# Two expert groups on one core: who loads group 1's gate and up weights, and when

## The chip, the cores and the metric

One core of one Trainium2 chip runs the whole program. The metric is the device time of one execution in microseconds, and the median of the runs counts. Lower is better.

## The reference

The program is a model of two layers on x of 2 x 2048 tokens by 256 channels, all in float32. The change lies in the first layer's feed-forward part, a mixture of experts in two groups of 32 experts each. Cut to what matters:

```python
def _moe_group(x2, router_w, wg, wu, wd, top_k):       # x2: 4096 x 256, top_k = 2
    scores = softmax(x2 @ router_w)                    # 32 experts
    expert_weights, expert_indices = lax.top_k(scores, top_k)
    order = argsort(flat_e); xs = x2[tok]              # 8192 rows sorted by expert
    gate = lax.ragged_dot(xs, wg, group_sizes)         # wg, wu: 32 x 256 x 128
    up = lax.ragged_dot(xs, wu, group_sizes)
    ys = lax.ragged_dot(silu(gate) * up, wd, group_sizes)   # wd: 32 x 128 x 256
    return zeros.at[tok].add(ys * flat_w[order])

out0 = _moe_group(x2, router_w0, wg0, wu0, wd0, 2)
out1 = _moe_group(x2, router_w1, wg1, wu1, wd1, 2)
out = (out0 * 2 + out1 * 2) / 4
```

Before it stand a layer norm and an attention, behind it the second layer: a gated delta attention with an MLP, and a soft mixture of experts.

## The kernel before

The kernel is written in phases. Each phase is a block in which every engine has its own program; the next phase begins when all five engines have come to the end of it. Engines talk through semaphores that count upwards.

Each group of experts is one phase, `phase_experts` with g = 0 and g = 1. The tokens of a group lie in DRAM in `slots_x`, sorted by expert and padded so that a tile of 128 rows belongs to one expert. There are always N = 96 tiles: 8192 / 128 = 64, and one more for each of the 32 experts. `tile_expert` holds the expert of each tile, which is known only at run time. Every expert has at least one tile, so tile t belongs to an expert not above t; and expert e can still own tile 64 + e but no later one.

A tile passes through the engines as follows (line numbers are the profile's). SyncE loads x for four tiles at once, 512 KB, into `xs`, which has room for eight (L1447). TensorE transposes a tile (L1514), ScalarE copies it from PSUM (L1547), TensorE multiplies by the expert's gate and up weights in `w_gu` (L1523), ScalarE applies silu (L1551), VectorE multiplies by up (L1570), TensorE transposes again (L1530), VectorE copies (L1574), TensorE multiplies by the down weights (L1536), ScalarE copies to `y` (L1560), and SyncE stores four tiles at once (L1456).

`staged` skews the steps of a tile over successive rounds: in round r TensorE does the first step of tile r, the second of tile r − 1, and so on. Some rounds at the start and the end are written out one by one, with constants as tile numbers; those between run in a hardware loop whose body holds `unroll` rounds, 8 on TensorE. How many rounds stand written out at the start is normally the number of stages less one, 3 on TensorE; the argument `alone` sets another number, and in group 1 TensorE has `alone=E + 1`, 33.

There is one buffer `w_gu` (8 MB over all partitions) for both groups. Group 0's content is loaded long before, in `phase_route` (L1378). Group 1's content is loaded in group 1's own phase by SyncE: `load_chunk` (L1439) loads four experts with 4 DMAs of 256 KB; there are 8 chunks. `load` issues chunk 0 behind the x load of tiles 0 to 3, and chunks 1 to 7 behind the x load of tiles 4 to 7, so that SyncE's program order is: x load, 4 weight DMAs, x load, 28 weight DMAs, x load, and so on. TensorE waits for chunk t / 4 ahead of the gate-up of tiles 0, 4, 8 to 28, which it can do because these rounds are written out.

The down weights have a buffer each. Group 1's go into `z_sb`, in one DMA of 4 MB that GpSimd issues in group 0's phase (L1472), after it has scattered group 1's tokens to `slots_x` with 64 indirect DMAs (L1352), which begin when tile 20 of group 0 has passed. Behind that DMA GpSimd's program for group 0 ends. In group 1's phase GpSimd gathers group 0's results, 64 indirect DMAs with a multiplication and an addition each (L1479, L1486, L1491).

Of the kernel before, what the change touches and what calls it, by code (L numbers as in the profile page):

```python
# [989 lines left out]
def phase_route(nc, sems, x, o_sb, out_w, out_b, routers, x1_sb, xn_sb, lg_sb, top_val, top_idx, ident,  # L990
# [3 lines left out]
    with Phase(nc, "route", sems) as ph:  # L994
# [42 lines left out]
        @block.sync  # L1037
        def _(sp):
            x_landed.prime(sp)
            sp.dma_start(w_in[:, :, :], out_w.rearrange("(c p) d -> p c d", p=P)).then_inc(consts_in, 16)  # L1040
            sp.dma_start(bias[:, 0, :], row_broadcast(out_b)).then_inc(consts_in, 16)
            for g, r in enumerate(routers):
                sp.dma_start(r_w[:, :, g * E:(g + 1) * E], r.rearrange("(k p) e -> p k e", p=P)).then_inc(consts_in, 16)

            def load(t, p):
                sp.wait_ge(x1_ready.sem, x1_ready.before(t))
                hold(sp, gate)
                sp.dma_start(x_in[:, p, :, :], x[bass.ds(t * GP, GP), :].rearrange("(n q) c -> q n c", q=P)).then_inc(x_landed.sems[p], 32)
            staged(sp, N, load)
            load_gate_up(sp, w_gu, *first_experts[:2], w_landed)  # L1050

        @block.gpsimd
        def _(pool):
# [325 lines left out]


CHUNK = 4
BACKS = 6
LOOPS_RUNNING = 20


def phase_experts(nc, sems, g, w_gu, w_d, next_w_d, weights, next_down, w_landed, down_landed, xn_sb, pos, scattered,
                  slots_x, slots_y, tile_expert, x1_sb, weight, ident):


# [5 lines left out]
    with Phase(nc, f"experts{g}", sems) as ph:  # L1395
# [12 lines left out]
        if g:  # L1408
# [1 line left out]
            back_landed = [ph.sem(f"back_landed{i}", soft=True) for i in range(BACKS)]  # L1410
            back_scaled = ph.sem("back_scaled")
            back_added = ph.sem("back_added")
        chunk_landed = [ph.sem(f"chunk_landed{c}") for c in range(E // CHUNK if g else 0)]
        x_landed = ph.transfers("x_landed")
        turned = ph.steps("turned", ahead=2 * GT)
        x_ready = ph.steps("x_ready")
# [11 lines left out]
        def _(sp):  # L1428
# [3 lines left out]
            if not g:  # L1432
                sp.dma_start(w_d[:, :, :], wd.rearrange("e h d -> h e d")).then_inc(down_landed[g], 16)

            def load_chunk(c):
                own = slice(c * CHUNK, (c + 1) * CHUNK)
                for k in range(KD):
                    for i, w in enumerate((wg, wu)):
                        sp.dma_start(w_gu[:, k, own, i, :],  # L1439
                                     w[own, k * P:(k + 1) * P, :].rearrange("e p h -> p e h")).then_inc(chunk_landed[c], 16)  # L1440

            sp.wait_ge(scattered[g], 16 * SCATTERS)

            def load(t, p):
                sp.wait_ge(turned.sem, turned.at(t * GT - GT - 1))
                hold(sp, gate)
                sp.dma_start(xs[:, p * GT:(p + 1) * GT, :],  # L1447
                             slots_x[bass.ds(t * GP + base, GP), :].rearrange("(n q) c -> q n c", q=P)).then_inc(x_landed.sems[p], 32)
                if g and isinstance(t, int) and t < 2:
                    for c in range(1) if t == 0 else range(1, E // CHUNK):  # L1450
                        load_chunk(c)

            def store(t, p):
                sp.wait_ge(y_ready.sem, y_ready.at(t * GT + GT - 1))
# [10 lines left out]
        def _(pool):  # L1465
            if g == 0:
                scatter_tokens(pool, 0, SCATTERS_EARLY, SCATTERS, xn_sb, pos, slots_x, scattered[0])

                pool.wait_ge(h_t_ready.sem, h_t_ready.at(LOOPS_RUNNING))
                scatter_tokens(pool, 1, 0, SCATTERS, xn_sb, pos, slots_x, scattered[1])  # L1470
                pool.wait_ge(scattered[1], 16 * SCATTERS)
                pool.dma_start(next_w_d[:, :, :], next_down.rearrange("e h d -> h e d")).then_inc(down_landed[1], 16)  # L1472
                return

            def fetch(i):
# [25 lines left out]
        def _(pe):  # L1501
            for s in (turned, gated, h_turned, down):
                s.prime(pe)
            if not g:
                pe.wait_ge(w_landed, 16 * 2 * KD)
            pe.wait_ge(down_landed[g], 16)

            def expert(t):
# [7 lines left out]

            def gate_up(t, p):
                e = expert(t)
                if g and isinstance(t, int) and t < E and t % CHUNK == 0:
                    pe.wait_ge(chunk_landed[t // CHUNK], 16 * 2 * KD)  # L1520
                pe.wait_ge(x_ready.sem, x_ready.at(t))
                for k in range(KD):
                    mm = pe.matmul(ps_g[p % 2][:, 0:2 * HID], x_t[:, p % 2, k, :],  # L1523
                                   w_gu[:, k, bass.ds(e, 1), :, :].rearrange("q a i h -> q (a i h)"),
                                   start=(k == 0), stop=(k == KD - 1))
                mm.then_inc(gated.sem, 1)
# [5 lines left out]
            def go_down(t, p):  # L1532
# [2 lines left out]
                pe.wait_ge(y_ready.sem, y_ready.before(t, 2))  # L1535
                pe.matmul(ps_y[p % 2][:, 0:D], h_t[:, p % 2, :], w_d[:, bass.ds(e, 1), :].rearrange("q a c -> q (a c)"),  # L1536
                          start=True, stop=True).then_inc(down.sem, 1)
            staged(pe, N, turn_x, gate_up, turn_h, go_down, unroll=2 * GT, alone=E + 1 if g else None)

        @block.scalar  # L1540
        def _(act):
# [1860 lines left out]
def two_layers(nc, t, out):  # L3402
# [13 lines left out]
    with ExitStack() as sems, ExitStack() as whole:  # L3416
# [2 lines left out]

        set_up, zeroed = [sems.enter_context(nc.semaphore(n)) for n in ("set_up", "zeroed")]  # L3420
        scattered = [sems.enter_context(nc.semaphore(f"scattered{g}")) for g in range(G)]
        w_landed = sems.enter_context(nc.semaphore("w_landed"))
        down_landed = [sems.enter_context(nc.semaphore(f"down_landed{g}")) for g in range(G)]
        ident = held(whole, "ident", [P, P])
        ident_bf = held(whole, "ident_bf", [P, P], BF16)
# [22 lines left out]
        with ExitStack() as ctx:  # L3448
# [9 lines left out]
                phase_slots(nc, layer, lg_sb, top_val, top_idx, weight, pos, tile_expert, z_sb, slots_x, scattered)  # L3458
            w_d = [held(ctx, "w_d", [P, E, D]), z_sb]
            for g in range(G):  # L3460
                phase_experts(nc, layer, g, w_gu, w_d[g], w_d[1], experts[g], experts[1][2], w_landed, down_landed, z_sb, pos, scattered,
                              slots_x, slots_y, tile_expert, x_sb, weight, ident)
        phase_combine(nc, layer, x_sb, z_sb, weight, pos, slots_y, attn1("Wq", "Wk", "Wv"), attn1("Wb", "Wg"),
                      *attn1("ln1_g", "ln1_b"), proj, ident)
# [60 lines left out]
```

## Time and profile before

| | us |
|---|---|
| median of 3 timed runs | 4291.71 |
| the three runs | 4291.42, 4291.71, 4296.32 |
| profiled execution, span from first to last instruction (its own whole time is not given apart from it) | 4296.5 |
| TensorE matmuls busy | 3510.7 |
| group 0's phase, from SyncE's first x load to that of group 1 | 2003.79 to 2298.80 |
| group 1's phase, from SyncE's first x load to the next phase's first load | 2298.80 to 2538.50 |

The profile is of one execution. All times in it are microseconds from the start of the span. A row of the timeline gives the start, the duration, the engine (PE is TensorE's matmul, PEld its weight load, DVE VectorE, ACT ScalarE, POOL GpSimd, SPq the queue of DMAs that SyncE issues), the line of the kernel, the operation, what it writes and reads, and in brackets how long the engine had been idle just before, with what ended that. A row of the windows gives for a stretch the busy time of each engine with the number of instructions, then the granted clock of TensorE as a share of 2.4 GHz, the mean busy share of the 16 DMA engines, and what they moved.

### The profile page before, as it was taken

The numbers are of one execution on the slowest core, as the hardware profiler recorded it, in microseconds if no ns is written. First come the engines' busy times: TensorE is split into PE (matmuls) and PEld (weight loads), VectorE is DVE, ScalarE is ACT, GpSimd is POOL, SyncE is SP. The second block draws the span as 40 slices with busy tenths as digits, with TensorE's granted clock in tenths as the row PEclk, the third lists the DMA queues.
The fourth block names the chain that finished last, engine by engine and source line by source line (L and its number), as shares of the span: only waits on it lengthen the run. The fifth ranks groups of instructions, "written<-read, shape, count | busy, mean of one in ns | idle before, by whom it ended". The sixth has DMA issues, their size and how long they took to land. (4 is left out here: it accounts for less than half of the span.)

```text
span 4296.5 us, 115371 instructions
## 1 busy us (share of the span) xinstructions
PE 3510.7 (82%) x41173; PEld 1852.0 (43%) x41175; DVE 2485.8 (58%) x5229; ACT 2102.7 (49%) x4024; POOL 1149.9 (27%) x2368
## 2 busy tenths in 40 slices
PE   8699999999999999732396977550869699898999
PEld 5232222322323222332264644440757566544678
DVE  7788888888888888580021238457245433235433
ACT  2488888888888888421143434320610022264322
POOL 1222222222222221124505844510533123210000
PEclk9799999999999999866698988555965599898999
DMA  1000000000000002534346533344723300233353
GB/s 53 7 6 6 6 6 7 6 6 6 6 7 6 6 6 89 189 102 139 136 137 195 161 118 124 122 140 150 246 84 75 86 15 0 84 135 125 108 188 125
DMA packets 288679, 345.07 MB, mean 80 GB/s; under 512 B 36768, under 2 KB 201632, under 8 KB 288544
## 3 DMA queue, kind: packets, MB, share of 16 engines
q1 hardware_dynamic: 254736, 297.27, 21.7%
q0 software_dynamic: 13328, 37.77, 2.7%
q10 hardware_dynamic: 20480, 8.40, 0.7%
q8 instruction: 64, 1.05, 0.1%
q14 instruction: 71, 0.58, 0.0%
HBM read 198.11 MB, written 135.79 MB: 78 GB/s over the span
## 5 line engine op out<-in xcount | busy, mean ns | idle before, releaser
L945 DVE TENSOR_REDUCE att_maxes<-att_ps_m 128x1 f32<-128x512 f32 x2048 | 1308.5, 686 | 230.9 <-PE att_ps_m L789 225.2
L900 ACT ACTIVATE att_prob<-att_ps_s 128x512 f32<-128x512 f32 x2048 | 1105.6, 599 | 222.5 <-PE att_ps_s L799 209.9
L799 PE MATMUL att_ps_s<-att_q_t,att_k_t 99*128 99x512 bf16 x2048 | 687.2, 386 | 8.7 <-ACT att_prob L900 7.9
L810 PE MATMUL att_ps_o<-att_prob,att_v_h 128*32 128x512 f32 x4096 | 546.4, 605 | 0.7 <-ACT att_prob L900 0.7
L787 PE MATMUL att_ps_m<-att_k_t,att_q_t 48*128 48x512 bf16 x1024 | 398.8, 389 | 16.3 <-DVE att_maxes L945 11.5
L789 PE MATMUL att_ps_m<-z_sb 48*128 48x512 bf16 x1024 | 399.3, 390 | 0.0
L787 PEld LDWEIGHTS att_ps_m<-att_k_t,att_q_t 48*128 48x128 bf16 x1024 | 94.6, 92 | 610.3 <-DVE att_maxes L945 509.8
L1570 DVE TENSOR_TENSOR experts_h<-experts_gs,experts_ps_g 128x128 f32<-128x128 f32 x192 | 55.3, 288 | 497.4 <-ACT experts_gs L1551 423.5
L698 POOL CAST att_max_parts<-att_neg_max 128x4 bf16<-128x4 f32 x128 | 24.9, 194 | 1154.1 <-DVE att_neg_max L952 1154.1
L799 PEld LDWEIGHTS att_ps_s<-att_q_t,att_k_t 99*128 99x128 bf16 x2048 | 157.7, 96 | 281.0 <-ACT att_prob L900 134.4
L1523 PE MATMUL experts_ps_g<-w_gu,experts_x_t 128*128 x768 | 225.1, 417 | 54.8 <-issue 41.0
L1514 PE MATMUL experts_ps_t<-ident,experts_xs 128*128 128x128 f32 x384 | 76.7, 284 | 136.3 <-DMA experts_xs<-slots_x 135.8
L1523 PEld LDWEIGHTS experts_ps_g<-w_gu,experts_x_t 128*128 128x128 f32 x768 | 135.7, 197 | 104.3 <-issue 90.6
L2673 ACT COPY mlp_o_t<-mlp_ps_ot 128x512 f32<-128x512 f32 x16 | 9.4, 587 | 346.2 <-PE mlp_ps_ot L2623 346.2
L1352 POOL DMA_INDIRECT slots_x<-z_sb,pos x128 | 128.9, 1007 | 126.0 <-DVE experts_h_t L1574 54.9
L1547 ACT COPY experts_x_t<-experts_ps_t 128x256 f32<-128x256 f32 x192 | 72.3, 377 | 171.2 <-issue 133.6
L1551 ACT ACTIVATE experts_gs<-experts_ps_g 128x128 f32<-128x128 f32 x192 | 53.3, 278 | 185.4 <-PE experts_ps_g L1523 149.1
L2304 ACT ACTIVATE mix_wide<-mix_tp_in,halves 128x256 f32<-128x256 f32 x128 | 54.9, 498 | 164.3 <-DMA mix_fac_in<-factors 152.7
L810 PEld LDWEIGHTS att_ps_o<-att_prob,att_v_h 128*32 128x32 f32 x4096 | 80.6, 108 | 117.4 <-issue 115.7
L1560 ACT COPY experts_y<-experts_ps_y 128x256 f32<-128x256 f32 x192 | 71.5, 372 | 111.6 <-PE experts_ps_y L1536 81.1
L1806 PE MATMUL comb_ps_p<-comb_w_s,comb_h_t 128*128 128x512 f32 (+1 forms) x256 | 102.8, 566 | 27.8 <-ACT comb_h_t L1831 19.4
L1514 PEld LDWEIGHTS experts_ps_t<-ident,experts_xs 128*128 128x128 f32 x384 | 54.5, 147 | 160.1 <-issue 122.0
(357 smaller groups left out, 6472.0 us busy)
## 6 DMA issues: line engine op xcount, KB each, us to landing
xf_t<-logits_t SPq DMA_DIRECT2D x16, 2048.0 KB, 8.5
slots_x<-zeros SPq DMA_DIRECT2D x97, 256.0 KB, 3.3
experts_xs<-slots_x SPq DMA_DIRECT2D x48, 512.0 KB
slots_y<-experts_y SPq DMA_DIRECT2D x48, 512.0 KB
logits_t<-sstat_logit SPq DMA_DIRECT2D x64, 256.0 KB
proj<-comb_pr SPq DMA_DIRECT2D x8, 1600.0 KB
mix_pr<-proj SPq DMA_DIRECT2D x32, 400.0 KB
gram_qk_in<-proj SPq DMA_DIRECT2D x32, 256.0 KB
```

What stands on the lines that cost most here:

```text
L787: pe.matmul(ps_m[bank(p, i)][:, :], q_t[0:LEADING, p, tile * P:(tile + 1) * P], k_t[0:LEADING, p, c * W:(c + 1) * W], start=True, stop=Tru ...
L789: pe.matmul(ps_m[bank(p, i + 1)][:, :], q_low[:, p, tile * P:(tile + 1) * P], k_low[:, p, (c + 1) * W:(c + 2) * W], start=True, stop=True) ...
L799: pe.matmul(ps_s[bank(p, i)][:, :], k_t[0:ROWS, p, tile * P:(tile + 1) * P], q_t[0:ROWS, p, chunk * W:(chunk + 1) * W], start=True, stop=T ...
L810: mm = pe.matmul(ps_o[i * VW:(i + 1) * VW, :], v_h[:, p, group * GK + i, :], prob[:, (j * GK + i) % (RING * GK), :], start=(group == 0), s ...
L900: nc.scalar.activation(prob[:, i % (RING * GK), :], ps_s[bank(p, i)][:, :], ACT.Exp, scale=SCALE).then_inc(expd.sem, 1)
L945: v.tensor_reduce(maxes[:, p, tile, c:c + 1], ps_m[bank(p, i)][:, :], X, ALU.max).then_inc(reduced.sem, 1)
L1352: pool.indirect_dma_start(out=slots_x, out_offset=bass.IndirectOffsetOnAxis(ap=pos[:, t, g, r:r + 1], axis=0), in_=xn_sb[:, t, :], in_offs ...
L1514: mm = pe.transpose(ps_t[p % 2][:, k * P:(k + 1) * P], xs[:, p, k * P:(k + 1) * P], ident[:, :])
L1523: mm = pe.matmul(ps_g[p % 2][:, 0:2 * HID], x_t[:, p % 2, k, :], w_gu[:, k, bass.ds(e, 1), :, :].rearrange("q a i h -> q (a i h)"), start= ...
L1547: nc.scalar.copy(x_t[:, p % 2, :, :].rearrange("q k n -> q (k n)"), ps_t[p % 2][:, 0:D]).then_inc(x_ready.sem, 1)
L1560: nc.scalar.copy(y[:, p, :], ps_y[p % 2][:, 0:D]).then_inc(y_ready.sem, 1)
L1806: mm = pe.matmul(ps_p[(t + i) % 3][:, a:b], h_t[:, k, i * P:(i + 1) * P], w_s[:, k, a:b], start=(k == 0), stop=(k == KD - 1))
```

## The change

SyncE's `load_chunk` and the eight semaphores `chunk_landed` go. In group 0's phase GpSimd, behind the DMA of the down weights, runs through the eight chunks: it waits until group 0's gate-up of tile `last_tile` of the chunk's last expert has been done (tiles 67, 71, ... 95), and then issues the same 4 DMAs of 256 KB into the same places of `w_gu`. The first seven chunks count on the semaphore `next_landed`, the last on `last_landed`. In group 1 TensorE waits for the first seven once, at the start; for the last it waits ahead of the gate-up of every tile whose position in the unrolled body of eight is 7, first at tile 7. `alone` goes, so that in group 1, too, TensorE has only 3 rounds written out and enters the loop then.

```diff
-            load_gate_up(sp, w_gu, *first_experts[:2], w_landed)
+            load_gate_up(sp, w_gu, *first_experts[:2], w_landed[0])
 ...
+CHUNKS = E // CHUNK
+def last_tile(e):
+    return T * TOPK // P + e
 ...
-        chunk_landed = [ph.sem(f"chunk_landed{c}") for c in range(E // CHUNK if g else 0)]
 ...
-            def load_chunk(c):
-                own = slice(c * CHUNK, (c + 1) * CHUNK)
-                for k in range(KD):
-                    for i, w in enumerate((wg, wu)):
-                        sp.dma_start(w_gu[:, k, own, i, :],
-                                     w[own, k * P:(k + 1) * P, :].rearrange("e p h -> p e h")).then_inc(chunk_landed[c], 16)
 ...
-                if g and isinstance(t, int) and t < 2:
-                    for c in range(1) if t == 0 else range(1, E // CHUNK):
-                        load_chunk(c)
 ...
                 pool.dma_start(next_w_d[:, :, :], next_down.rearrange("e h d -> h e d")).then_inc(down_landed[1], 16)
+                for c in range(CHUNKS):
+                    own = slice(c * CHUNK, (c + 1) * CHUNK)
+                    pool.wait_ge(gated.sem, gated.at(last_tile((c + 1) * CHUNK - 1)))
+                    for k in range(KD):
+                        for i, w in enumerate(next_gate_up):
+                            pool.dma_start(w_gu[:, k, own, i, :], w[own, k * P:(k + 1) * P, :].rearrange("e p h -> p e h")
+                                           ).then_inc(w_landed[1 if c < CHUNKS - 1 else 2], 16)
                 return
 ...
-            if not g:
-                pe.wait_ge(w_landed, 16 * 2 * KD)
+            pe.wait_ge(w_landed[g], 16 * 2 * KD * (CHUNKS - 1 if g else 1))
 ...
-                if g and isinstance(t, int) and t < E and t % CHUNK == 0:
-                    pe.wait_ge(chunk_landed[t // CHUNK], 16 * 2 * KD)
+                if g and p == 2 * GT - 1:
+                    pe.wait_ge(w_landed[2], 16 * 2 * KD)
 ...
-            staged(pe, N, turn_x, gate_up, turn_h, go_down, unroll=2 * GT, alone=E + 1 if g else None)
+            staged(pe, N, turn_x, gate_up, turn_h, go_down, unroll=2 * GT)
 ...
-        w_landed = sems.enter_context(nc.semaphore("w_landed"))
+        w_landed = [sems.enter_context(nc.semaphore(n)) for n in ("w_landed", "next_landed", "last_landed")]
```

## Rows read from the trace of the kernel before

**Rows 1.** The page: the span, and TensorE's busy tenths in 40 equal slices.
```profile
span 4296.5 us, 115371 instructions
...
PE   8699999999999999732396977550869699898999
```

**Rows 2.** Windows, columns in the first line: stretches of both groups.
```profile
core 0: us, PE busy (x) PEld busy (x) DVE busy (x) ACT busy (x) POOL busy (x), PEclk, DMA share, GB/s
...
2158.00:2272.00 114.00, 102.65 (x472) 72.36 (x470) 25.61 (x105) 48.75 (x156) 0.00 (x0) 1.00 0.38 120
...
2321.00:2341.00 20.00, 0.00 (x0) 0.00 (x0) 0.02 (x1) 0.29 (x1) 17.57 (x20) 0.58 1.17 308
...
2057.00:2149.00 92.00, 24.57 (x71) 14.31 (x71) 4.37 (x16) 7.34 (x24) 63.18 (x65) 0.56 0.40 139
...
2141.00:2158.00 17.00, 10.64 (x39) 8.01 (x39) 2.54 (x11) 4.98 (x16) 0.27 (x1) 0.63 0.90 308
...
2056.00:2065.00 9.00, 8.34 (x39) 5.80 (x38) 2.05 (x8) 3.05 (x10) 6.01 (x7) 1.00 0.60 189
```

**Rows 3.** Timeline, SyncE's DMA queue at group 1's start.
```profile
2298.80 0.41 SPq L1447 DMA_DIRECT2D experts_xs<-slots_x  x1
...
2333.80 0.78 SPq L1439 DMA_DIRECT2D w_gu<-in_L_ffn_wu  x1
2335.04 1.08 SPq L1447 DMA_DIRECT2D experts_xs<-slots_x  x1
```

**Rows 4.** Timeline, TensorE's matmuls in group 1.
```profile
2302.83 1.08 PE L1514 MATMUL experts_ps_t<-ident,experts_xs 128*128 128x128 f32 x4 [8.24 <-DMA experts_xs<-slots_x]
...
2307.16 2.07 PE L1523 MATMUL experts_ps_g<-w_gu,experts_x_t 128*128 x4 [3.25 <-DMA w_gu<-in_L_ffn_wu]
...
2341.42 0.69 PE L1514 MATMUL experts_ps_t<-ident,experts_xs 128*128 128x128 f32 x2 [20.62 <-DMA experts_xs<-slots_x]
...
2342.17 2.07 PE L1523 MATMUL experts_ps_g<-w_gu,experts_x_t 128*128 x4
...
2380.58 1.13 PE L1523 MATMUL experts_ps_g<-w_gu,experts_x_t 128*128 x4
```

**Rows 5.** Timeline, SyncE's DMA queue: ends of runs of stores and loads.
```profile
2003.79 10.61 SPq L1447 DMA_DIRECT2D experts_xs<-slots_x  x3
2022.27 0.43 SPq L1456 DMA_DIRECT2D slots_y<-experts_y  x1
...
2158.87 0.41 SPq L1456 DMA_DIRECT2D slots_y<-experts_y  x1
...
2272.66 0.41 SPq L1456 DMA_DIRECT2D slots_y<-experts_y  x1
...
2349.18 0.33 SPq L1456 DMA_DIRECT2D slots_y<-experts_y  x1
...
2388.98 0.41 SPq L1456 DMA_DIRECT2D slots_y<-experts_y  x1
...
2406.20 0.41 SPq L1456 DMA_DIRECT2D slots_y<-experts_y  x1
...
2512.89 0.41 SPq L1456 DMA_DIRECT2D slots_y<-experts_y  x1
...
2538.50 0.39 SPq L1646 DMA_DIRECT2D comb_w_in<-in_L_attn_Wq  x1
```

**Rows 6.** Timeline, GpSimd: w_d's load, its next instruction, its last in group 1.
```profile
2139.51 1.77 POOL L1472 DMA_DIRECT2D z_sb<-in_L_ffn_wd  x1 [1.74 <-DMA slots_x<-z_sb,pos]
...
2299.20 1.02 POOL L1479 DMA_INDIRECT experts_back<-slots_y,pos  x1 [157.93 <-POOLq L150]
...
2495.04 0.73 POOL L1491 TENSOR_TENSOR x_sb<-experts_back,x_sb 128x256 f32<-128x256 f32 x1
```

**Rows 7.** Timeline at group 0's end: the last gate-up and the last store.
```profile
2290.36 1.13 PE L1523 MATMUL experts_ps_g<-w_gu,experts_x_t 128*128 x4
...
2295.09 0.40 SPq L1456 DMA_DIRECT2D slots_y<-experts_y  x1
```

More of the change, by code:

```diff
@@ L1381, with phase_experts @@
 CHUNK = 4
+CHUNKS = E // CHUNK
+def last_tile(e):
+    return T * TOPK // P + e
 BACKS = 6
 LOOPS_RUNNING = 20
-def phase_experts(nc, sems, g, w_gu, w_d, next_w_d, weights, next_down, w_landed, down_landed, xn_sb, pos, scattered,
+def phase_experts(nc, sems, g, w_gu, w_d, next_w_d, weights, next_gate_up, next_down, w_landed, down_landed, xn_sb, pos, scattered,
                   slots_x, slots_y, tile_expert, x1_sb, weight, ident):
@@ L3460, in two_layers @@
             for g in range(G):
-                phase_experts(nc, layer, g, w_gu, w_d[g], w_d[1], experts[g], experts[1][2], w_landed, down_landed, z_sb, pos, scattered,
+                phase_experts(nc, layer, g, w_gu, w_d[g], w_d[1], experts[g], experts[1][:2], experts[1][2], w_landed, down_landed, z_sb, pos, scattered,
                               slots_x, slots_y, tile_expert, x_sb, weight, ident)
```

## The prediction

> **What bounds the kernel now.** I read the page's slices first. The program is a row of phases that follow one another, and the change touches two of them, slices 19 to 24 of 40: the two expert groups. TensorE is at 9 tenths in slices 21 and 23; slice 20, in group 0, is at 3, and slice 22, where group 1 begins, at 6 [rows 1]. Next I read the windows of that part. In an undisturbed stretch of group 0 TensorE is busy 102.65 of 114.00 us at full clock while the DMA engines are busy 0.38 of the time and move 120 GB/s; from 2321 to 2341 us it is busy 0.00 of 20.00 us while the DMA engines are at 1.17 of their time and move 308 GB/s [rows 2]. So a tile is bounded by TensorE's stream, and the start of group 1 by transfers.
>
> The timeline says which transfers. SyncE issues group 1's first x load at 2298.80, the second shortly behind four weight DMAs, and then 28 more weight DMAs, the last at 2333.80; only then, at 2335.04, comes the load of tiles 8 to 11 [rows 3]. TensorE starts at 2302.83, waits 3.25 us for the first chunk of w_gu (2307.16), works through tiles 0 to 7, and then waits 20.62 us for that x load (2341.42) [rows 4]. The stall is not for weights: it is for an x load that stands behind them in SyncE's program order and shares the DMA engines with them. What the reader is to see is the bracket at the end of the two rows.
>
> **What it removes.** The two waits: 3.25 + 20.62 = 23.9 us. After the long one TensorE is granted 1.2 GHz for a while: the four matmuls of gate and up take 2.07 us there against 1.13 us at 2.4 GHz [rows 4], and this lasts about 3.5 us until all rows are back at the short durations; about half of it, 1.7 us, goes too. The slow spell at 2302.83, behind the change of groups, stays. Sum: 25.6 us. What is late next: TensorE's own stream, since the third x load can go out as soon as the first four tiles are turned, some 10 us ahead of its need.
>
> **What it adds in group 1: the loop.** TensorE's first 33 rounds are written out now; afterwards only 3 are, as in group 0, and the rest run in the loop of eight. SyncE's stores, one for four tiles, time this. Written out: from 2349.18 to 2388.98, five intervals, 7.96 us each. In the loop: from 2406.20 to 2512.89, twelve intervals, 8.89 us each [rows 5]. The difference is 0.93 us for four tiles, 0.23 us a tile; the 30 rounds from 3 to 32 cost 7.0 us. Bounds: 0 if the written-out form were not the cause (other engines run the same code in both stretches, so I take the full 7), and 8 if entering the loop costs one more round. The new wait on w_landed[2] stands before every eighth gate-up, some 12 times, long satisfied: under 0.05 us each, 0.5 us in all. It could only bind if the last chunk took over 15 us, for tile 7 is that far from the group's start.
>
> **What it adds in group 0: GpSimd's 32 DMAs.** GpSimd has nothing to do there: it idles 157.93 us before its first gather of group 1 [rows 6]. Its wait is on tile 67, then on every fourth tile to 95; nothing else is queued behind these waits in that phase. One DMA of 256 KB costs GpSimd at least what an indirect one does, 65 of them busy for 63.18 us in [rows 2] or 0.97 us, and at most what the whole w_d load of 4096 KB took, 1.77 us [rows 6]; with 0.30 us between them, 1.27 to 2.07 us each. A chunk is 5.1 to 8.3 us of issuing in the 8.75 us that four tiles take (from 2158.87 to 2272.66, thirteen intervals [rows 5]). I take 1.27, as a DMA here is a sixteenth of w_d's. A chunk adds 1 MB per 8.75 us, 120 GB/s, to the 120 GB/s that flow: 240, under the 308 that flowed while w_d landed beside running tiles from 2141 to 2158 [rows 2]. x loads have a buffer of four tiles, 8.75 us, ahead; the one that was issued at 2335.04 amid saturated engines landed in 6.4 us [rows 3, 4]. So the seven chunks before the last are covered; I put 0.5 us for all, between 0 and 3.
>
> The last chunk has no cover of that sort. Its wait ends with the last gate-up of group 0, which starts at 2290.36 and ends at 2291.5; four DMAs at 1.27 us are issued by 2296.6. The last store goes out at 2295.09 and group 1's first load at 2298.80 [rows 3, 7], so GpSimd reaches the end of the phase 1.5 us or so before SyncE does. The last store shares the engines with one or two of these DMAs; 0.25 to 0.5 MB at 300 GB/s is 0.8 to 1.7 us. I take 1.0, with 0 and 3 as ends. At group 1's start the first x load no longer shares the engines; but group 0's, which had them nearly to itself, also took 4 us, so nothing is gained.
>
> **Sum.** 25.6 − 7.0 − 0.5 − 0.5 − 1.0 = 16.6 us. A second way to the same: group 0 has the form that group 1 will have. From its first load to its first store it took 18.5 us (2003.79 to 2022.27); add 20 intervals of 8.89 and the 25.6 us that lie between store 21 and the next phase's first load (2512.89 to 2538.50) [rows 5]: 221.9 us from 2298.80, that is 2520.7 instead of 2538.50, 17.8 us less; less 1.5 for the tail gives 16.3. I take 16.5. GpSimd's own work in group 1, 64 gathers with two sums each, ends at 2495.04 + 0.73 [rows 6] and would still be over by 2519, so it becomes no bound. The phases behind start earlier and are otherwise unchanged.
>
> The profiled span is 4296.5 us, at the level of the slowest of the three timed runs, 4296.32; it would become 4280.0. On the median, 4291.71 − 16.5 = 4275.2 us.
>
> **The skill against the trace.** GpSimd's indirect DMAs took it 0.97 us each in the stretch from 2057 to 2149, with VectorE at work beside them [rows 2]. The Trainium skill, page "SBUF — State Buffer", section "SBUF: two separate sides", warns that a DMA issued from GpSimd waits for its descriptors while VectorE copies in a two-port mode, and gives 3100 ns where 620 would do. By that rule four DMAs would end near 2304, and the phase some 6 us late: 4281. No row here shows it for a direct DMA beside tiles, and VectorE's copies in this phase read PSUM. It is a reason for rival (b), which is priced from rows.
>
> **Rivals.**
> (a) *GpSimd's issuing stalls the tiles, slower.* It happened once in this kernel. From 2057 to 2149 GpSimd scattered group 1's tokens, 65 DMAs busy 63.18 us, and TensorE was busy only 24.57 of 92.00 us at a clock of 0.56 [rows 2]; by group 0's stores about 75 us were lost over 80 us of issuing, 0.94 us per us. Were the same to hold for 32 direct DMAs of 1.27 us, 40.6 us of issuing would cost 38 us: 4291.7 − 16.5 + 38 = 4313. It decides from 0.5 us lost per DMA on. Against it: the w_d load, as large as four chunks, ran from 2141 to 2158 and the tiles came back to speed within it [rows 2]; and in the scatters' first 8 us, more than a chunk's burst, TensorE was still busy 8.34 of 9.00 us [rows 2]. For it: nobody in the trace says what held the engines then. Chance 0.13.
> (b) *GpSimd late at the end of group 0.* At w_d's price per DMA it is done at 2291.5 + 8.3 = 2299.8, about 2 us past the present end, and the landing of the last store slips with it; with the bounds of both, 4277 to 4283. Chance 0.10.
> (c) *The bytes were the bound, not the order.* The change then moves the stall into the last 28 tiles: 8 MB at 308 GB/s are 27 us of DMA time, and with what the tiles need they must fit in 61 us. They fit (0.38 + 0.45 of the time), so this needs x loads that take over 8.75 us in each chunk; 2 us for each of seven would give 4289. Chance 0.05.
> (d) *The loop costs nothing.* 4275.2 − 7 = 4268. Chance 0.09.
> The forecast itself, with its bounds of 4270 to 4281, has 0.63.
>
> **How the numbers follow.** Low end 4266: (d) with the small terms at 0. High end 4289: all of (b), most of (c). Outside lies mainly (a). A difference of 0.2%, 8.6 us, is about what a measurement of this kernel can tell from none: faster is below 4283.1, and holds the forecast, (d), and most of (b): 0.79. Same: what is left of (b) and (c) and a weak form of (a): 0.09. Slower, above 4300.3: 0.12.
>
> **What would show it.** Right: SyncE issues x loads in group 1 from its start without weight DMAs between; no wait of TensorE over 1 us on x or w_gu there; store intervals near 8.9 us from the first on (the loop's price); intervals of group 0 from tile 67 on still near 8.75; the next phase's first load near 2522. Wrong: group 0's intervals stretch while GpSimd issues (a, c); the gap between the last store of group 0 and the first load of group 1 grows beyond 3.7 us by more than 1 (b); intervals near 8.0 in the first third of group 1 (d).

## The result, and the profile after

The changed kernel takes 4261.35 us (median of 4 runs, 4257.32 to 4261.59) against 4292.62 us for the kernel before, measured beside it (4291.42 to 4296.32). The ratio is 0.9923 with a 95% interval of 0.9909 to 0.9937. It is 31.3 us faster; 16.5 were forecast, and the time lies 4.7 us below the low end of the range.

The profiled execution after took 4261.56 us with a span of 4259.8 us, 36.7 less than the span before [rows 1]. The page, TensorE's busy tenths in 40 slices, and the DMA queues:

```profile
span 4259.8 us, 115443 instructions
...
PE   8699999999999999742488967541869699898999
...
q1 hardware_dynamic: 237840, 288.88, 21.0%
q0 software_dynamic: 15888, 46.16, 3.4%
```

The 6 in group 1's beginning is gone (slices 20 to 24 are now 4, 8, 8, 9, 6), and 8.39 MB have moved from the hardware queue to GpSimd's software queue (before: 297.27 and 37.77 MB). SyncE's DMA queue after, from group 0's last store to the next phase:

```profile
2283.86 0.40 SPq L1453 DMA_DIRECT2D slots_y<-experts_y  x1
2289.30 10.67 SPq L1447 DMA_DIRECT2D experts_xs<-slots_x  x3
2307.92 0.42 SPq L1453 DMA_DIRECT2D slots_y<-experts_y  x1
...
2482.78 0.42 SPq L1453 DMA_DIRECT2D slots_y<-experts_y  x1
...
2508.91 0.39 SPq L1649 DMA_DIRECT2D comb_w_in<-in_L_attn_Wq  x1
```

The three x loads now follow one another at 2289.30, with no weight DMA between, where [rows 3] had 36 us between the first and the third. TensorE at the same place:

```profile
2293.26 1.09 PE L1517 MATMUL experts_ps_t<-ident,experts_xs 128*128 128x128 f32 x4 [9.89 <-DMA experts_xs<-slots_x]
2294.46 2.07 PE L1526 MATMUL experts_ps_g<-w_gu,experts_x_t 128*128 x4
```

The first gate-up has no bracket: both waits of [rows 4], 3.25 and 20.62 us, are gone. Stage by stage, from the first SyncE load of a phase to that of the next (`phase_route`, which ends the attention, and the phase that computes the slots lie ahead of group 0; the two experts' phases follow; the slots phase has no such load ahead of group 0 and is counted from its first instruction, an IOTA of GpSimd). Lengths of phases here and below are good to 0.1 us:

| us | start of route | route | slots | group 0 | group 1 | from there to the end | span |
|---|---|---|---|---|---|---|---|
| before | 1771.7 | 108.6 | 123.5 | 295.0 | 239.7 | 1758.0 | 4296.5 |
| after | 1773.5 | 97.6 | 123.6 | 294.6 | 219.6 | 1750.9 | 4259.8 |

So 20.1 us come from group 1, 0.4 from group 0, 7.1 from behind both groups, and 9.1 from ahead of them (route is 11.0 shorter; the part ahead of it is 1.8 longer and slots 0.1), where the change touches no line. The experiments are about these four numbers.

### The profile page after: what moved, and what is told of

The parts are those of the page before. It is cut to its first block and busy times, and to the rows that moved or that the text cites. A ratio compares the mean times of both kernels' runs of the same rounds, so it can differ in the third digit from the quotient of the medians.

```text
span 4259.8 us, 115443 instructions
## 1 busy us (share of the span) xinstructions
PE 3501.3 (82%) x41173; PEld 1843.0 (43%) x41175; DVE 2478.1 (58%) x5229; ACT 2103.7 (49%) x4024; POOL 1174.4 (28%) x2400
## 5 line engine op out<-in xcount | busy, mean ns | idle before, releaser
L787 PE MATMUL att_ps_m<-att_k_t,att_q_t 48*128 48x512 bf16 x1024 | 399.1, 390 | 16.2 <-DVE att_maxes L945 11.5
L1554 ACT ACTIVATE experts_gs<-experts_ps_g 128x128 f32<-128x128 f32 x192 | 53.4, 278 | 191.0 <-PE experts_ps_g L1526 154.4
L3098 PE MATMUL disp_ps_s<-disp_probs,z_sb 128*128 128x512 f32 x256 | 116.9, 601 | 4.8 <-ACT disp_probs L3145 4.8
```

The source lines that it names most:

```text
L787: pe.matmul(ps_m[bank(p, i)][:, :], q_t[0:LEADING, p, tile * P:(tile + 1) * P], k_t[0:LEADING, p, c * W:(c + 1) * W], start=True, stop=Tru ...
L3098: mm = pe.matmul(ps_s[:, k, n * GP:(n + 1) * GP], xf_sb[:, t, k * P:(k + 1) * P], probs[:, t % 2, n * GP:(n + 1) * GP], start=t % ST == 0, ...
```

## The experiments

There are four sets, each with runs of the kernel before beside it: e1 to e4, e5 to e8, e9 and e10, e11 and e12. A ratio is the time over that of the kernel before in the same set, with its 95% interval. In the first, third and fourth set the kernel before takes 4231 to 4232 us instead of 4292; that difference lies nearly all in group 0, and every kernel has it (last section).

**e1 and e2: both kernels again.** No edit. They ask whether the 9 and the 7.1 us come again.

> The kernel before, unchanged, to see what moves between executions of one program. The span fell by 36.7 us with the change: 9.5 us before the experts begin (route phase), 0.0 in group 0, 20.1 in group 1, 7.1 behind it. Theory A (route and the phases behind fall differently by small shifts in time, the program before being steadily on the bad side): the ratio to before is 1.000 within 0.001, and in the profile the route phase from its first x load to the slots phase is again near 106 us, VectorE's first normalisation again takes 3.4 us for four instructions. Theory B (chance of one execution): the phase is near 97 us in this profile or the times spread by over 5 us. Group 1 takes 239.7 us in both.

> The changed kernel, unchanged. Theory A: ratio 0.992 to 0.994 again, route phase near 97 us, group 1 at 219.6 us. Theory B: the route phase or the mix phase is as long as before in this profile while group 1 stays at 219.6, and the time is then near 4271.

e1: 4231.85 us, ratio 1.0003 [0.9994, 1.0013]. e2: 4196.49 us, ratio 0.9917 [0.9901, 0.9934]. By stage, e1 against e2: route 106.9 and 97.3, group 1 240.0 and 219.2, behind the groups 1754.7 and 1754.8. So route's 10 us and group 1's 20.8 belong to the changed program, and the 7.1 us behind do not: that stretch took 1750.9 to 1761.2 us in the fourteen executions profiled, in no relation to which of the two programs ran. Of theory B one sign did come: e1's ten times spread over 15.1 us (4222.55 to 4237.69), and the profiled one is the fastest of them. Its group 0 is short, 223.8 us against 233.0 in e2; the 9 us lie in the stretch in which GpSimd scatters, not in the one in which it issues the chunks (the six store intervals before the last run of stores take 53.4 us in e1, 52.2 in e2).

**e3: the change with the written-out rounds given back.** Against e2 it is the loop's price by itself, and against e1 the worth of the moved loads by itself.

```diff
-            staged(pe, N, turn_x, gate_up, turn_h, go_down, unroll=2 * GT)
+            staged(pe, N, turn_x, gate_up, turn_h, go_down, unroll=2 * GT, alone=E + 1 if g else None)
```

> The changed kernel with TensorE's first 33 rounds of group 1 written out again, nothing else. My step (the loop costs 0.23 us a tile, 7.0 us): group 1 takes 212 to 213 us instead of 219.6, store intervals 7.9 to 8.1 us for stores 2 to 7 and 8.7 behind. Rival (the written-out form was not the cause; in the kernel before SyncE and the loads set the pace there): store intervals stay near 8.74 and group 1 at 219 to 220. The outer phases may shift by up to 10 us either way, so group 1's own length is the measure.

4207.71 us, ratio 0.9949 [0.9932, 0.9965]. Group 1 takes 214.6 us, only 4.6 less than in e2, where 30 rounds at 0.23 us would be 7. SyncE's stores in e3 (the first, the seventh, and those at either end of twelve later intervals):

```profile
2253.27 0.42 SPq L1453 DMA_DIRECT2D slots_y<-experts_y  x1
...
2300.28 0.42 SPq L1453 DMA_DIRECT2D slots_y<-experts_y  x1
...
2317.44 0.42 SPq L1453 DMA_DIRECT2D slots_y<-experts_y  x1
...
2424.29 0.41 SPq L1453 DMA_DIRECT2D slots_y<-experts_y  x1
```

Written out, six intervals take 7.84 us each; in the loop, twelve take 8.90. In the changed kernel the loop takes (2482.78 − 2307.92) / 20 = 8.74. The written-out part is as fast as forecast, and the loop behind it is slower than the same loop entered after 3 rounds: 0.16 us over the 14 intervals behind the seventh store give back 2.2 us. Against e1, which has the same written-out rounds and the loads still in group 1, it is 25.3 us shorter (239.9 to 214.6): that is what the moved loads are worth. With 33 rounds written out TensorE's body of eight begins at another tile, against those of ScalarE and VectorE, than with 3; e7 tests that. And e3's route phase took 107.3 us again, so the time as a whole is longer than e2's although group 1 is shorter.

**e4: the kernel before, with the chunks spread.** SyncE still loads all weights in group 1; the order changes: chunks 0 and 1 behind the first x load, one chunk behind each of the next six. For this SyncE has its first eight rounds written out.

```diff
-                if g and isinstance(t, int) and t < 2:
-                    for c in range(1) if t == 0 else range(1, E // CHUNK):
+                if g and isinstance(t, int) and t < E // CHUNK - 1:
+                    for c in (0, 1) if t == 0 else (t + 1,):
 ...
-            staged(sp, N // GT, load, idle, store)
+            staged(sp, N // GT, load, idle, store, alone=E // CHUNK if g else None)
```

> The kernel before, its 8 chunks still loaded by SyncE in group 1, but spread: two behind the first x load and one behind each of the next six, so that no x load stands behind more than 8 weight DMAs. If order in SyncE's queue was what cost (my step): the 20.6 us wait is gone, the first wait on w_gu stays at 3 to 5 us, written-out rounds run at 7.9 to 8.5 us per four tiles, group 1 takes 214 to 222 us. If the bytes were the bound (rival c): TensorE waits for x or w_gu at each chunk, 20 us or more in sum, and group 1 stays over 230 us.

4208.35 us, ratio 0.9948 [0.9931, 0.9964]. Group 1 takes 219.2 us, the same as in e2. TensorE's waits on transfers at group 1's start in e4 (total, times, longest):

```profile
PE experts_ps_t L1514 <- DMA experts_xs<-slots_x: 8.3, 1, 8.3
PE experts_ps_g L1523 <- DMA w_gu<-in_L_ffn_wu: 3.2, 1, 3.2
```

The wait of 20.62 us is gone with the same bytes, in the same phase, from the same queue; the one for the first chunk stays. The order in SyncE's program was the cause. e4 keeps the faster written-out rounds and pays for it with 3.2 us of wait and with longer intervals (8.19 us over stores 2 to 8, where e3 has 8.01). Its route phase took 107.0 us, so it has group 1's part of the gain and not the other.

**e5 and e6: a guard in the route phase.** In the trace of before, in `phase_route`, GpSimd adds a bias to a whole x load (L1062) while VectorE normalises tiles (L214). VectorE, then GpSimd, then TensorE, before:

```profile
1791.24 3.42 DVE L214 TENSOR_SCALAR route_xn<-route_x,route_mv,route_rstd 128x256 f32<-128x256 f32 x4 [1.13 <-POOL route_rstd L1066]
```

```profile
1791.84 2.34 POOL L1062 TENSOR_TENSOR route_x_in<-route_x_in,route_bias 128x1024 f32<-128x1024 f32 x1 [0.64 <-DMA route_x_in<-in_L_attn_x]
```

```profile
1794.79 1.55 PE L1099 MATMUL route_ps_x<-ident,route_xn 128*128 128x128 f32 x8 [2.54 <-DVE route_xn L214]
1797.09 3.67 PE L1105 MATMUL route_ps_l<-route_r_w,route_turn_t 128*128 128x64 f32 x16 [0.75 <-ACT route_turn_t L1133]
```

and the same three after:

```profile
1793.19 1.38 DVE L214 TENSOR_SCALAR route_xn<-route_x,route_mv,route_rstd 128x256 f32<-128x256 f32 x4 [1.13 <-POOL route_rstd L1066]
```

```profile
1794.51 2.37 POOL L1062 TENSOR_TENSOR route_x_in<-route_x_in,route_bias 128x1024 f32<-128x1024 f32 x1 [1.35 <-DMA route_x_in<-in_L_attn_x]
```

```profile
1794.71 1.09 PE L1099 MATMUL route_ps_x<-ident,route_xn 128*128 128x128 f32 x8 [0.50 <-DVE route_xn L214]
1796.61 1.99 PE L1105 MATMUL route_ps_l<-route_r_w,route_turn_t 128*128 128x64 f32 x16 [0.81 <-ACT route_turn_t L1133]
```

Before, GpSimd's addition starts 0.60 us into VectorE's four instructions, and these take 3.42 us instead of 1.38; TensorE idles 2.54 us and comes back at half its clock (3.67 us for the 16 matmuls where 1.99 would do; the clock granted from 1796 to 1806 is 0.50, and 1.00 after). After, the x load lands 0.7 us later against the rest, GpSimd starts when VectorE has just finished, and neither happens. The guard keeps them apart: GpSimd's addition to a load waits until VectorE has normalised the load two before, the one it met.

```diff
             def add_bias(t, p):
                 pool.wait_ge(x_landed.sems[p], x_landed.at(t, p))
+                pool.wait_ge(norm.sem, norm.before(t))
```

e5 is the kernel before with this line, e6 the changed one with it.

> The kernel before, with one wait more in the route phase: GpSimd's bias addition on a token tile (L1062) waits until VectorE has normalised the tile two earlier (L214), so that the two can't run at the same moment. Collision theory (the 10 us between 97 and 107 us of route are that addition falling into VectorE's first normalisation, which then takes 3.4 instead of 1.4 us, and TensorE's half clock behind the gap): route takes 96 to 99 us, the whole 8 to 11 us less, ratio 0.9975. Rival (the long form has another cause, such as the landing of x itself or the start of TensorE's clock): route stays at 106 to 109 us and the ratio at 1.000 or above.

> The changed kernel with the same one wait in the route phase. Collision theory: the changed kernel escaped the collision already, so nothing is gained: route 96 to 99 us, and the ratio between this and the kernel before with the wait is the change's own worth, 20 us in group 1 alone: near 0.9950. Rival: the change is worth 30 us or more beside that wait too (ratio between the two 0.9925).

e5: 4280.53 us against 4294.16, ratio 0.9966 [0.9954, 0.9978], route 97.9 us. e6: 4257.85 us, ratio 0.9916 [0.9902, 0.9929], route 92.9. The guard alone, on the kernel before, gives 13.6 us at the medians, and 10.7 us in route (108.6 to 97.9). VectorE's line 214 in e5 and then in before: count, shortest, median and longest in ns, first and last start.

```profile
L214 DVE TENSOR_SCALAR route_xn<-route_x,route_mv,route_rstd x32: 405/409/416, 1793.7 to 1861.0; 128x256 f32<-128x256 f32 x32
```

```profile
L214 DVE TENSOR_SCALAR route_xn<-route_x,route_mv,route_rstd x32: 401/409/2468, 1791.2 to 1869.9; 128x256 f32<-128x256 f32 x32
```

The long ones are gone (416 ns instead of 2468). The phase has eight loads, and line 214 has four instructions for each; they take 1.38 us, or 3.4 to 3.5 where GpSimd's addition falls into them. In before six of the eight are long, in the changed kernel two, the third and the fifth (longest instruction 2506 ns), and in e5 and e6 none. So e6 gains in route too, 4.7 us against after; the expectation saw nothing to gain there. With the guard in both, the change is worth 22.7 us (0.9947): group 1 239.5 against 218.5 us. The Trainium skill, page "SBUF — State Buffer", section "SBUF: two separate sides", says that VectorE and GpSimd share a pair of SBUF ports under an exclusive lock, which the first of the two holds for its whole instruction, if VectorE's is in a two-port mode or has two inputs in SBUF. By that rule a VectorE instruction that comes second would stand still until GpSimd's addition is over, and the trace agrees: in before the third of the four starts at 1791.89, 0.05 us behind the addition, and takes 2468 ns; the addition is over at 1794.18, the instruction at 1794.36. The mode that it ran in stands in no row.

One thing the guard does not explain: e5's route is still 5.0 us longer than e6's. Granted clock and busy times over twice 10 us, e5 and then e6:

```profile
1792.00:1802.00 10.00, 8.47 (x45) 7.18 (x43) 7.48 (x34) 4.69 (x7) 5.60 (x4) 0.80 0.33 104
1802.00:1812.00 10.00, 8.69 (x35) 7.11 (x36) 4.52 (x27) 2.87 (x5) 1.15 (x1) 0.69 0.02 7
```

```profile
1792.00:1802.00 10.00, 7.84 (x51) 6.59 (x50) 8.35 (x43) 4.89 (x7) 5.81 (x4) 1.00 0.20 64
1802.00:1812.00 10.00, 8.20 (x53) 7.20 (x52) 7.34 (x41) 4.89 (x7) 3.36 (x2) 1.00 0.18 52
```

TensorE is granted 0.80 and 0.69 of full speed in e5 and 1.00 in e6, though from 1789 us on the matmuls have the same order, durations and idle times in both until then. Before that they differ in one group, 16 matmuls in 5.73 us in e5 and in 6.04 in e6, behind a first wait of 18.34 and 17.43 us; whether this decides it is open.

**e7: 35 written-out rounds instead of 33.** 35 leaves the remainder 3 by 8, as the 3 rounds of the changed kernel and of ScalarE do; 33 leaves 1. (VectorE has two steps and so one round written out, not 3 as the expectation has it; that is the same in all these kernels.)

```diff
-            staged(pe, N, turn_x, gate_up, turn_h, go_down, unroll=2 * GT)
+            staged(pe, N, turn_x, gate_up, turn_h, go_down, unroll=2 * GT, alone=E + 3 if g else None)
```

> The changed kernel with 35 instead of 3 rounds written out (before: 33). With 33, TensorE's loop of eight begins two rounds later in its cycle than ScalarE's and VectorE's (33 is 1, 3 is 3 modulo 8), so the engines jump back at different rounds. If that is why stores in the loop stood at 8.9 us in the kernel before and in e3, but at 8.74 in the changed kernel: store intervals 7.8 us up to store 7, then 8.7 us, group 1 at 212 to 213 us. If gathers or the written-out part set that rate: 8.9 us again and group 1 at 214 to 215.

4264.91 us, ratio 0.9937 [0.9924, 0.9951]. Group 1 takes 211.8 us, 6.7 less than in e6 in the same set. Its stores at either end of twelve loop intervals:

```profile
2378.66 0.41 SPq L1453 DMA_DIRECT2D slots_y<-experts_y  x1
...
2484.11 0.12 SPq L1453 DMA_DIRECT2D slots_y<-experts_y  x1
```

That is 8.79 us an interval, 0.11 less than in e3 with its 33 rounds and close to the 8.74 of the changed kernel. Over the same stores of all executions the loop takes 8.84 to 8.90 us with 33 rounds (before, e1, e3, e4, e5), 8.76 and 8.79 with 35 (e10, e7) and 8.70 to 8.77 with 3 (after, e2, e6, e9, e11, e12). The rate goes with the remainder; only two remainders were tried, and the number of written-out rounds also moves the loop within the program, which is not told apart. With the remainder kept, 32 written-out rounds are worth 6.7 us, 0.21 a tile (e10 against e6: 5.6). The time as a whole is 7.1 us above e6's although group 1 is shorter, for route takes 107.0 us here and 92.9 there.

**e8: all but the last rounds written out, with the guard.** `alone=N - 13` in group 1, and the line of e6.

> The changed kernel with the wait in the route phase and nearly all rounds of TensorE in group 1 written out (83, then one pass of the loop). By the rate of the written-out part, 7.83 us for four tiles instead of 8.74: 80 tiles by 0.23 us are 18 us off group 1, 219.4 to 201 or 202 us. GpSimd's gathers, which end 196 us behind the start of the group, would be close to the bound: at best 200 us. Rival: so many instructions no longer arrive in time and the rate falls back to 8.5 us or worse behind some round: group 1 over 210.

4248.2 us, ratio 0.9891 [0.9875, 0.9906]. Group 1 takes 202.3 us: 16.2 less than in e6, which has the guard too. The whole time is only 9.7 us less, since the phases behind the groups took 1761.2 us here and 1752.5 in e6; the profiled execution lies within 2 us of the median, so this isn't one odd execution. Its cause is open.

**e9: the kernel before with TensorE's loop.** Nothing is moved to GpSimd. `alone` goes, as in the change; TensorE can then wait only once, for all eight chunks.

```diff
-                if g and isinstance(t, int) and t < E and t % CHUNK == 0:
-                    pe.wait_ge(chunk_landed[t // CHUNK], 16 * 2 * KD)
+                if g and isinstance(t, int) and t == 0:
+                    for landed in chunk_landed:
+                        pe.wait_ge(landed, 16 * 2 * KD)
 ...
-            staged(pe, N, turn_x, gate_up, turn_h, go_down, unroll=2 * GT, alone=E + 1 if g else None)
+            staged(pe, N, turn_x, gate_up, turn_h, go_down, unroll=2 * GT)
```

> The kernel before, its chunks loaded by SyncE in group 1 as before, but with only 3 rounds of TensorE written out; since the loop can't wait chunk by chunk, TensorE waits for all eight chunks ahead of the first gate-up of group 1. It does the loop's part of the change alone. Group 1: the chunks land near 40 us behind its start instead of 4, and from there 96 tiles at 8.74 us for four, so 250 to 256 us (before: 239.7). Route phase: if it is the length of TensorE's program that decides how route falls (the changed kernel with 3 rounds written out had 97 us, the same with 33 or 35 had 107), route is 97 to 98 us here with nothing moved to GpSimd. If the weight loading or something else of the change decides: 107 us.

4229.72 us, ratio 0.9995 [0.9986, 1.0005]. TensorE in group 1:

```profile
2262.62 2.07 PE L1524 MATMUL experts_ps_g<-w_gu,experts_x_t 128*128 x4 [35.27 <-DMA w_gu<-in_L_ffn_wu]
```

It waits 35.27 us for the weights, group 1 takes 254.5 us, 14.5 more than in e1, and the time as a whole is unchanged, because route takes 93.0 us, 13.9 less than in e1 and less than either theory gave. So route's short form comes from a kernel that differs from the one before only in TensorE's program for group 1, a phase that begins 357 us after route has ended. GpSimd's new DMAs are not needed for it, and with 33 or 35 rounds written out (e3, e7) they do not bring it.

**e10: guard and 35 rounds.** The edits of e6 and e7 together.

> The changed kernel with 35 rounds written out and with the wait in the route phase. Without that wait it had route at 107 us and group 1 at 211.8. Two things made route long in it: the collision of GpSimd's addition with VectorE's normalisation, and TensorE's clock granted at 0.72 behind it. The kernel before with the wait kept the dip of the clock (0.80 and 0.69) and took 97.9 us, the changed one with the wait had none and took 92.9. If the dip goes with the program and not with the collision: 97 to 98 us. If it goes with the collision or the weight loading: 93 us.

4191.78 us, ratio 0.9902 [0.9886, 0.9919]; route 93.0 us, group 1 212.8. A program with many rounds written out, then, has the short route phase too once the guard is in, at a clock of 1.00; e5's lower clock doesn't come from the written-out form as such.

**e11 and e12: length at the end of the program.** 400 empty instructions behind the last phase, on TensorE in e11 and on SyncE in e12. They ask whether the mere length of a program moves the x load in route.

```diff
+        with nc.Block() as block:
+            @block.tensor
+            def _(pe):
+                for _ in range(400):
+                    pe.nop()
```

> The changed kernel with 400 empty instructions behind its last phase on TensorE, about as many as 30 written-out rounds have. They run when everything else is over and lengthen the end by up to 25 us; what counts is the route phase, 2000 us earlier. If it is the sheer length of TensorE's program (and with it where things lie in memory) that decides whether GpSimd's third addition falls into VectorE's first normalisation: the four normalising instructions take 3.4 us and route 105 to 108 us, as in the programs with 33 and 35 rounds. If the length does not decide: 1.4 us, and route 93 to 98 us.

> The same 400 empty instructions on SyncE instead of TensorE. If any program's length decides: route 105 to 108 us here too. If TensorE's alone does, or none: 93 to 98 us, and the normalisation takes 1.4 us.

e11: 4199.11 us (of 2 runs), ratio 0.9923 [0.9894, 0.9951], route 94.2. e12: 4200.44 us (of 2 runs), ratio 0.9926 [0.9897, 0.9955], route 96.4. The short form stays: 400 instructions more at the program's end do not bring the long one.

Over the ten profiled executions without a guard there is no exception: where TensorE has 33 or 35 rounds of group 1 written out (before, e1, e3, e4, e7), GpSimd waited 0.60 to 0.78 us for that x load, hit VectorE, and route took 106.9 to 108.6 us; where it has 3 (after, e2, e9, e11, e12), GpSimd waited 1.28 to 1.42 us and route took 93.0 to 97.6. The number of loads in which the two meet orders the lengths:

| loads that meet, of eight | executions | line 214 busy, us | route, us |
|---|---|---|---|
| 6, the first six | before, e1, e3, e4, e7 | 23.2 to 23.4 | 106.9 to 108.6 |
| 2 | after, e2, e12 | 15.2 to 15.3 | 96.4 to 97.6 |
| 1 | e11 | 13.2 | 94.2 |
| 0 | e9; with the guard e6, e8, e10 (e5, at the lower clock) | 11.1 | 92.9 to 93.1 (97.9) |

Where the first load meets, the next five meet too. So route's 10 us between before and after are four meetings more. What in the code of a later phase moves the landing of a load of 512 KB by 0.7 us is not settled: an edit between route and group 1 that changes length alone was not tried.

## Why the prediction was wrong, step by step

**What bounds the kernel: right.** The start of group 1 was bounded by the order in SyncE's queue, as read from the two rows and their bracket. e4 shows it: another order, the same bytes, and the wait of 20.62 us is gone. Rival (c), the bytes as the bound, falls with it.

**The two waits and the clock, 25.6 us: right.** No wait over 1 us on x or w_gu is left in group 1 behind its first load, and e3 against e1, where only the loads' place differs, gives 25.3 us. The first wait for x is 9.89 us long where it was 8.24 [rows 4]; this is the change of phases and belongs to the tail, below.

**The loop, 7.0 us: right for the rounds, wrong for the rest.** The step took the difference over the 30 rounds and left the rest of the group as it was; e2 against e3 gives 4.6 us for the whole of it, the 0.5 us put down for the new wait included. The 0.23 us a tile over the 30 rounds are confirmed twice: written-out intervals of 7.84 us stand against 8.74 in the changed kernel's loop, 0.23 a tile, and e7 with 32 rounds more than e6 is 6.7 us shorter in group 1, 0.21 a tile. What failed shows in the second way to the sum: 20 intervals of 8.89 us, taken from [rows 5]. That was the rate of a loop entered after 33 rounds. The changed kernel enters it after 3 and runs at 8.74, 2.9 us less over 20 intervals. With that, 17.8 becomes 20.7, and the first load to the first store (18.6 us instead of 18.5) and the last stretch (26.1 instead of 25.6) take 0.6 off: 20.1, what was measured. The clue stood in the same trace: group 0, in that very form, had 8.75 us for four tiles [rows 5], and the prediction used it for group 0 only.

**GpSimd's DMAs: too dear, and it made no difference.** They were put at 1.27 us each, 5.1 a chunk. GpSimd, the last chunk and the first instruction of group 1, after:

```profile
2280.56 0.75 POOL L1475 DMA_DIRECT2D w_gu<-in_L_ffn_wg  x1 [4.79 <-PE experts_ps_g L1526]
2281.30 0.75 POOL L1475 DMA_DIRECT2D w_gu<-in_L_ffn_wu  x1
2282.04 0.75 POOL L1475 DMA_DIRECT2D w_gu<-in_L_ffn_wg  x1
2282.78 0.75 POOL L1475 DMA_DIRECT2D w_gu<-in_L_ffn_wu  x1
2289.71 1.03 POOL L1483 DMA_INDIRECT experts_back<-slots_y,pos  x1 [6.19 <-POOLq L150]
```

They take 0.75 us each and follow one another without the 0.30 between, in all chunks but one: 3.0 us a chunk. The lower bound was drawn at an indirect DMA, and a direct one of 256 KB lies below it. GpSimd is done at 2283.53, ahead of the last store at 2283.86, and idles 6.19 us, so rival (b) falls.

**Contention, 0.5 us: nothing.** The window over the whole issuing, after (all 32 DMAs lie in it):

```profile
2218.00:2284.00 66.00, 59.74 (x271) 41.49 (x269) 14.95 (x61) 28.16 (x90) 23.82 (x32) 1.00 0.78 231
```

231 GB/s flow, where 240 were worked out, the DMA engines are at 0.78, and TensorE is busy 59.74 of 66.00 us at full clock. Of its time that is 0.91, where the undisturbed stretch of before has 102.65 of 114.00, 0.90 [rows 2]. The six store intervals from the sixteenth store of group 0 on take 8.70 us each (2217.41 to 2269.62) and took 8.72 before (2228.64 to 2280.94). Rival (a) falls: 24 us of issuing cost the tiles nothing. In e1 the scatters themselves hardly held the tiles (last section), so GpSimd's issuing alone is not what held them in before.

**The tail, 1.0 us: 1.7.** From the last store to group 1's first load it is 5.44 us (2283.86 to 2289.30) against 3.71 [rows 7, 3]. It is within the bounds given. The gap is 3.71 or 3.72 us in the five executions without weight DMAs from GpSimd and 5.06 to 6.26 in the nine with them. That growth was named as the sign of (b), but GpSimd was not the late one; that the last store lands later beside four weight DMAs is the reading that is left, and no row shows the landing. Group 0 as a whole is no longer for it (294.6 against 295.0). Two of the prediction's readings here are off by its own numbers and changed nothing: GpSimd's forecast end, 2296.6, is 2.2 us ahead of 2298.80, not 1.5, and 2299.8 in (b) is 1.0 us behind it, not 2.

**What was not in the sum: the phases ahead, 9 us.** This is the step that failed most. The prediction said that phases behind start earlier and are otherwise unchanged, and did not speak of those ahead: it put them at nothing without a reason, as if a phase that no line touches could not change. Route changed by 11.0 and 9.6 us in the two pairs without the guard, and by 5.0 in the pair with it; in the pairs without it two loads meet in place of six. Of the 14.8 us between 31.3 and 16.5, 4.0 come from groups 0 and 1 (20.5 measured, 16.5 forecast), some 9 from ahead of them, and the rest is within what executions differ by. The groups alone, with 20.5 us, would have given 4271 us, inside the range. Why the program's change moves the loads of route stays open.

**The sign and the shares.** Faster had 0.79, and that held. Rival (d), 4268, had the nearest time, for a reason that was not the right one: the loop is not free, it costs 4.6 us (e2 against e3).

## What to carry to other kernels

Ask of a wait whether it is for bytes or for a place in a queue: if the load that is waited for was issued behind a row of others that nobody needs yet, spreading them (e4) or moving them to an idle queue brings the same. Take a loop's rate from a stretch that has the form the changed code will have, here group 0, rather than from the nearest stretch of the same phase. A phase that the diff leaves alone can move when VectorE and GpSimd meet on SBUF by a margin of half a microsecond: look for such a pair where the longest instruction of a line takes a multiple of its median, and keep them apart by a wait, so that the time no longer hangs on it. Count the meetings, not only the first.

## What the runs showed of the hardware

Two engines that meet on SBUF: VectorE's instruction of 0.41 us took 2.47 us when GpSimd's of 2.34 us began beside it, and six such meetings with their consequences cost 10.7 us of the route phase (before against e5), or 14 to 16 against the kernels without any at full clock (93 us).

TensorE's granted clock went two ways behind nearly the same matmuls and idle times: 0.80 and then 0.69 in e5, 1.00 in e6, with one earlier group at 5.73 against 6.04 us. Route is 5.0 us longer in e5.

A loop body of eight tiles cost 8.70 to 8.79 us for four tiles when TensorE entered it after 3 or 35 rounds, 8.84 to 8.90 after 33, and 7.8 to 7.9 written out, once the weights were loaded ahead (e3, e7, e8, e10).

Group 0 took 292 to 296 us in six of the fourteen executions profiled (before, after, e5 to e8) and 224 to 235 in the other eight, with either form of the kernel, each set of runs being of one kind. The difference lies in the stretch in which GpSimd scatters. The same window as in [rows 2], in e1:

```profile
2057.00:2149.00 92.00, 81.15 (x364) 55.92 (x363) 19.68 (x81) 38.03 (x122) 62.06 (x64) 1.00 0.71 228
```

TensorE is busy 81.15 us there and was 24.57; GpSimd's 64 DMAs take the same 62 us. So the stall that rival (a) was built on is no property of the kernel alone; what makes it come in some sets of runs and not in others is open.
